# An adaptive-norm and expert network on one core: the first stage's side work reordered (ternary weights, routing, first loads)

## What is computed

```
h  = x @ W_base.T + b + 2 * lora(x; As, Bs, cond)          # 8 adapters of rank 16, weighed per batch row
xn = layernorm(h) * gamma + beta
s  = max|xn| / 127;  xq = round(xn / s) * s                # one scale over the whole tensor
delta = 0.7 * mean|w|;  mask = |w| > delta
alpha = sum(|w| * mask) / max(sum(mask), 1)
x  = x + xq @ (alpha * sign(w) * mask).T                   # ternary weight

w, sel = top2(softmax(cond));  w = w / sum(w)              # router: 2 of 8 experts for each batch row
y  = sum_e w_e * mlp_e(x) + shared_mlp(x)                  # gelu(x Wg) * (x Wu) @ Wd, hidden 512
x  = x + quantised_gated_ffn(y)                            # global maxima between its steps
```

## Time and profile before

| | |
|---|---|
| time of the profiled execution | 493.8 us |
| its span | 491.9 us |
| median of three runs | 493.7 us |
| TensorE busy over the span | 390.9 us (79%) |
| VectorE / ScalarE / GpSimd busy | 336.2 / 267.8 / 254.5 us |
| TensorE busy, 0 to 68 us | 52.5 us |
| VectorE busy, 0 to 68 us | 39.8 us |
| VectorE busy in 28 to 44 us | 15.9 of 16 us |

### The profile page before, as it was taken

The page is one execution under the profiler, slowest core; times in us unless marked ns, Lnnn a source line. Parts: engine busy times, 40 slices in busy tenths (PEclk is TensorE's granted clock), DMA queues, the critical chain, the costliest instruction groups (busy, mean ns, idle before and its releaser), DMA issues.

```text
span 491.9 us, 8519 instructions
## 1 busy us (share of the span) xinstructions
PE 390.9 (79%) x2556; PEld 343.3 (70%) x2556; DVE 336.2 (68%) x564; ACT 267.8 (54%) x403; POOL 254.5 (52%) x444
## 2 busy tenths in 40 slices
PE   3998949999999999999999999798587860000297
PEld 2786636779999999999999998566265640000197
DVE  2697458557888767777677676467465778979643
ACT  3575558755454454544545446354365679659360
POOL 2667426886767756657566102566233018967140
PEclk9998758999999999999999999899588995555599
DMA  8899900228777777676777506200000000000012
GB/s 287 331 311 322 333 3 0 82 91 279 240 249 262 242 264 256 233 278 237 253 261 233 193 23 267 87 1 1 0 0 0 1 0 0 0 1 0 0 65 107
DMA packets 30786, 71.26 MB, mean 145 GB/s; under 512 B 3475, under 2 KB 19606, under 8 KB 25494
## 3 DMA queue, kind: packets, MB, share of 16 engines
...
q10 hardware_dynamic: 1472, 0.20, 0.3%
...
HBM read 55.12 MB, written 15.60 MB: 144 GB/s over the span
## 4 chain that ended last, share of the span: by engine, by line
PE 63%; DVE 18%; ACT 8%; POOL 5%; DMA 4%; issue 2%; ACTq 0%; POOLq 0%; DVEq 0%
PE ps L180 46%; PE ps L734 10%; DVE S L198 7%; DVE G L189 4%; PE ps L737 4%; DMA G<-yscr,sidx 3%; PE ps L177 2%; DMA wbr<-in_L_cond_W_base_dram 2%; ACT ps L186 1%; ACT G L186 1%; POOL Hl L189 1%; POOL XCl L189 1%; ACT U L186 1%; ACT C_i L186 1%; DVE G L195 1%
## 5 line engine op out<-in xcount | busy, mean ns | idle before, releaser
L689 POOL CAST xg<-XT 128x64 fp32r x312 | 115.4, 417 | 59.5 <-PE ps L180 55.8
L186 ACT ACTIVATE Gb<-ps 128x512 f32<-128x512 f32 x110 | 65.7, 597 | 106.4 <-PE ps L180 105.9
L180 PE MATMUL ps<-xg,Wr 128*128 128x256 f32 x936 | 120.0, 284 | 0.0
L189 DVE TENSOR_TENSOR HbS<-Gb,ps 128x512 f32<-128x512 f32 x110 | 75.5, 687 | 63.5 <-PE ps L180 61.8
L180 PEld LDWEIGHTS ps<-xg,Wr 128*128 128x128 f32 x936 | 114.3, 190 | 0.1
L186 ACT ACTIVATE Hh<-HbS 128x512 fp32r<-128x512 f32 x110 | 69.0, 628 | 13.8 <-DVE HbS L189 13.6
L734 PE MATMUL ps<-WD,Hh 128*128 x312 | 74.3, 328 | 0.0
L737 PE MATMUL ps<-WD,Hl 128*128 x312 | 69.4, 223 | 0.0
L189 DVE TENSOR_TENSOR Hl<-HbS,Hh 128x512 fp32r<-128x512 f32 x90 | 64.5, 726 | 2.6
L737 PEld LDWEIGHTS ps<-WD,Hl 128*128 128x128 f32 x312 | 59.8, 192 | 0.0
L734 PEld LDWEIGHTS ps<-WD,Hh 128*128 128x128 f32 x312 | 59.0, 189 | 0.0
(11 more groups left out here) (183 smaller groups left out, 699.8 us busy)
## 6 DMA issues: line engine op xcount, KB each, us to landing
...
yscr<-Yb SPq DMA_DIRECT2D x39, 128.0 KB, 2.7
...
```

Of the source, the lines that this page charges most:

```text
L180: return lambda e: e.matmul(o_, l, r, start=start, stop=stop, skip_group_check=True)
L186: return lambda e: e.activation(o_, i_, func, **kw)
L189: return lambda e: e.tensor_tensor(o_, a, b, op)
L689: k_xg[i] = pool.do(lambda e, s=s: e.tensor_copy(xg[:, i % XR, :, T * s:T * s + T], XT[:, :, :, bass.ds(regb[i][s], 1)].rearrange("p a t o ...
```

## The change

Four things are done, all in the first stage:

1. On ScalarE's transfer queue the order is now `wbr`, `fwr`, `bsr`; `fwr` leaves SyncE's queue. `wbr` gets a place in SBUF of its own beside `grow`.
2. In round 1 the adapter products of tile 0 come ahead of the products of `wbr` and `grow` on TensorE, and `hs` ahead of `WbTl` on VectorE.
3. The ternary chain moves from rounds 5 to 7 into rounds 0 and 1. Mask and masked value come from one operation each (`tpos`, `tsc` and `tneg`, `tsc2`, with -1 in `tneg`), there are four sums instead of two, and the two halves are added in PSUM by two products with `identF`. These and the product of `ones` with the sums stand in round 2 of TensorE. `tern` and `alpha` are made in round 3.
4. `Pm` is made at the end of round 4 (in round 5 before), its product stands in round 5 (6 before), and `ordI` in round 6 (7 before).

```diff
--- before.py
+++ after.py
...
+        tsc2 = at("tsc2", [128, 128], F32)
...
-        l_bs = act.dma(lambda e: e.dma_start(bsr[:, :].rearrange("o (e r) -> o e r", e=E), Bs.rearrange("e o r -> o e r")), s_in[4], 1)
         l_wb = act.dma(lambda e: e.dma_start(wbr[:, :], Wb), s_in[6], 1)
+        l_fw = act.dma(lambda e: e.dma_start(fwr[:, :], fw), s_in[2], 1)
+        l_bs = act.dma(lambda e: e.dma_start(bsr[:, :].rearrange("o (e r) -> o e r", e=E), Bs.rearrange("e o r -> o e r")), s_in[4], 1)
...
             tok["w01"] = dve.do(stt(S[:, 38:40], S[:, 34:36], 1.0 / 12, S[:, 36:38], MUL, ADD), d_)
+            d_f = dve.do(red(S[:, 10:11], fwr[:, :], ADD, True), l_fw)
             yield True
+            p_f = pe.do(mm(bank[6][:, 16:17], ones[:, :], S[:, 10:11], True, True), d_f)
             pe.do(mm(bank[6][:, 0:8], tri[:, :], S[:, 64:72], True, True), d4, k_tri, sig=False)
             p_ = pe.do(mm(bank[6][:, 8:16], ones[:, :], S[:, 64:72], True, True))
+            yield
+            d_ = dve.do(ts(S[:, 44:45], bank[6][:, 16:17], 0.7 / 16384, None, MUL), p_)
+            dve.do(cp(S[:, 72:80], bank[6][:, 0:8]), p_)
+            dve.do(ts(S[:, 80:88], bank[6][:, 8:16], 1.0 / SL, 0.5 - 0.5 / SL, MUL, ADD), p_)
+            d6 = dve.do(ts(S[:, 45:46], S[:, 44:45], -1.0, None, MUL), d_)
+            dve.do(ts(tpos[:, :], fwr[:, :], S[:, 44:45], None, ALU.is_gt), d_)
+            dve.do(stt(tsc[:, :], fwr[:, :], S[:, 44:45], fwr[:, :], ALU.is_gt, MUL), d_)
+            d_n = dve.do(ts(tneg[:, :], fwr[:, :], S[:, 45:46], -1.0, ALU.is_lt, MUL), d6)
+            d7 = dve.do(stt(tsc2[:, :], fwr[:, :], S[:, 45:46], fwr[:, :], ALU.is_lt, MUL), d6)
+            yield
+            dve.do(red(S[:, 46:47], tpos[:, :], ADD), d7)
+            dve.do(red(S[:, 47:48], tsc[:, :], ADD))
+            dve.do(red(S[:, 140:141], tneg[:, :], ADD))
+            d7 = dve.do(red(S[:, 141:142], tsc2[:, :], ADD))
+            yield
+            d7 = dve.do(tt(S[:, 46:48], S[:, 46:48], S[:, 140:142], SUB), d7)
             yield True
...
+            pe.do(mm(bank[6][:, 18:20], ones[:, :], S[:, 46:48], True, True), d7, sig=False)
+            pe.do(mm(bank[6][:, 384:512], tpos[:, :], identF[:, :], True, False), tok["w2"], sig=False)
+            p_t = pe.do(mm(bank[6][:, 384:512], tneg[:, :], identF[:, :], False, True), d_n)
...
+            tok["tern"] = dve.do(cp(tern[:, :], bank[6][:, 384:512]), p_t)
+            d_a = dve.do(ts(S[:, 140:141], bank[6][:, 18:19], 1.0, None, ALU.max), p_t)
             for i in range(1, E):
...
+                if i == 1:
+                    d_a = dve.do(lambda e: e.reciprocal(S[:, 141:142], S[:, 140:141]), d_a)
+                if i == 3:
+                    tok["alpha"] = dve.do(tt(S[:, 142:143], S[:, 141:142], bank[6][:, 19:20], MUL), d_a)
...
-            yield True
+            yield
             dve.do(cp(bcF[:, :], bcI[:, :]), k_bc)
             d_P = dve.do(stt(Pm[:, :], iof[:, :], S[:, 43:44], tmpP[:, :], ALU.is_equal, ADD), (dve.sem, dve.n - 1))
...
             yield True
-            p_ = pe.do(mm(bank[6][0:1, 0:NSLOT], bcF[:, :], Pm[:, :], True, True), d_P)
...
-            yield True
+            p_ = pe.do(mm(bank[6][0:1, 0:NSLOT], bcF[:, :], Pm[:, :], True, True), d_P, tok["alpha"])
+            yield True
             tok["ord"] = dve.do(cp(ordI[:, :], bank[6][0:1, 0:NSLOT]), p_)
-            pe.do(mm(bank[6][:, 18:20], ones[:, :], S[:, 46:48], True, True), d_, tok["ord"], sig=False)
-            p_ = pe.do(tr(bank[6][:, 384:512], tpos[:, :], identF[:, :]), tok["w2"])
...
-            if n == 1:
-                p_ = pe.do(mm(bank[5][:, 0:128], wbr[:, :], ctr[:, :], True, True), l_wb, k_ctr)
...
-            fill(2)
+            if n != 1:
+                fill(2)
...
             if n == 1:
+                p_ = pe.do(mm(bank[5][:, 0:128], wbr[:, :], ctr[:, :], True, True), l_wb, k_ctr)
...
+                fill(1)
                 p_ = pe.do(mm(AV[:, 0:128], bsr[:, :], ctr[:, :], True, True), l_bs)
```

More of the change, by code:

```diff
@@ L121, in program @@
         stg = at("stg", [128, 8, 512], F32)
-        wbr = at("wbr", [128, 128], F32)
         asr = at("asr", [128, 128], F32)
@@ L152, in program @@
         grow = at("grow", [1, 3, 128], F32)
+        wbr = at("wbr", [128, 128], F32)
         assert off[0] <= RQ
@@ L237, in program @@
         l_a0 = act.dma(lambda e: e.dma_start(asr[:, :], As.rearrange("e r c -> (e r) c")), s_in[1], 1)
+        l_wb = act.dma(lambda e: e.dma_start(wbr[:, :], Wb), s_in[6], 1)
+        l_fw = act.dma(lambda e: e.dma_start(fwr[:, :], fw), s_in[2], 1)
         l_bs = act.dma(lambda e: e.dma_start(bsr[:, :].rearrange("o (e r) -> o e r", e=E), Bs.rearrange("e o r -> o e r")), s_in[4], 1)
-        l_wb = act.dma(lambda e: e.dma_start(wbr[:, :], Wb), s_in[6], 1)
         act.do(acp(S[0:1, 15:16], S4[0:1, 40:41], ACT.Exp), d_one)
@@ L247, in program @@
             l_gb = sp.dma(lambda e, k=k, v=v: e.dma_start(grow[0:1, k, :], v.rearrange("(a n) -> a n", a=1)), s_in[5], k + 1)
[L248 to L251, removed]
+        for n in range(8):
             load_w(n)
@@ L350, in route @@
             d_ = dve.do(stt(S[:, 96:104], S[:, 96:104], float(SL), S[:, 72:80], MUL, ADD), d_)
-            yield True
-            p_f = pe.do(mm(bank[6][:, 16:17], ones[:, :], S[:, 10:11], True, True), d_f)
             for i in range(1, E - 1):
@@ L463, in program @@
             if n == 1:
+                p_ = pe.do(mm(bank[5][:, 0:128], wbr[:, :], ctr[:, :], True, True), l_wb, k_ctr)
+                a_ws[0] = act.do(acp(WbTh[:, :], bank[5][:, 0:128]), p_)
+                d_ws[0] = dve.do(tt(WbTl[:, :], bank[5][:, 0:128], WbTh[:, :].bitcast(F32), SUB), a_ws[0])
+                for k in range(3):
+                    p_ = pe.do(mm(AZ[:, k:k + 1], grow[0:1, k, :], S4[0:1, 40:41], True, True), l_gb, d_one, sig=(k == 2))
+                d_ = dve.do(cp(S[:, 8:10], AZ[:, 0:2]), p_)
+                d_bb = dve.do(cp(S[:, 143:144], AZ[:, 2:3]), p_)
+                fill(1)
                 p_ = pe.do(mm(AV[:, 0:128], bsr[:, :], ctr[:, :], True, True), l_bs)
```

7 lines of the change are left out of this document (1 added, 6 removed).

## The result

The changed kernel takes 499.06 us, the median of five runs from 498.0 to 500.36. The kernel before takes 493.7 beside it (five runs, 489.41 to 496.85). The ratio is 1.0139, with a 95% interval of 1.009 to 1.0188, so the change makes the kernel 4.4 to 9.3 us slower. The ratio compares fast runs alone and leaves the one of 496.85 us out, which is why it gives 6.9 us where the medians lie 5.4 apart. The profiled execution of after took 499.06 us with a span of 497.3, against 493.8 and 491.9: the span is 5.4 us longer. The forecast of 497.3 us had the direction and lay 1.8 us short of this median; by the ratio the loss is 6.9 us where 3.6 were forecast.

The account below looks back on a forecast made before the run. TensorE was taken to bound the first stage, whose delays reach the end whole. Terms of +1.7 (front and ternary), +4.8, -4.6 and +1.7 gave +3.6 us, so 497.3 us, range 490.8 to 500.5.

Parts of the forecast that it names:

- front: Start up to round 2: splits behind `stg` still set the pace, so new load and work order win only -0.3 us.
- ternary wait and products: Round 2: TensorE waits 1.1 us for the ternary sums, then three new products take 0.9 us.
- order product: Round 5: TensorE waits 4.1 us for `Pm`, and its product of 0.69 us comes to this round; +4.8 us.
- recovery: Round 5's correction to round 9: no product waits for `ordI`, undisturbed pace if the clock stays high; -4.6 us.
- clock: Round 5: TensorE's granted clock falls to 0.50 behind the longer wait, in place of round 7's fall; +1.7 us.
- wait for `Pm`: Round 5: TensorE asks for `Pm` 11.4 us behind round 3's base product, ready at 15.5, so waits 4.1 us.
- `Pm` is in time: Faster rival: VectorE loses little to splits in rounds 3 and 4, clock holds; -2.2 us, 491.5, or 489; chance 0.22.
- a short wait and no fall: No-change rival: a 2.5 us wait for `Pm` in round 5, clock holds or falls briefly; +0.4 us, 494.1; chance 0.24.
- late first rise of the clock: Slower rival: the wait at 19.0 us makes TensorE's clock rise one round later; +2 to the forecast, 499.5; chance 0.16.

Follow-up runs that it names:

- e2: The changed kernel with `Pm`'s product moved to round 6 and `ordI` to round 7; 491.97 us, ratio 0.9996.
- e9: The changed kernel with 13 unused products of 512 columns on TensorE ahead of `Pm`'s product in round 5; 496.6 us, ratio 1.0109.
- e1: The changed kernel with `bsr` loaded ahead of `wbr` and `fwr` on ScalarE's queue; 498.82 us, ratio 1.016.
- e4: The changed kernel with the three ternary products in round 3 instead of 2, `tern` and `alpha` later in round 3; 496.72 us, ratio 1.0099.
- e5: The kernel before with only the order part: `Pm` made at the end of round 4, its product in round 5; 498.92 us, ratio 1.0137.
- e3: The changed kernel with `bcF` and `Pm` ahead of the two `etI` operations on VectorE in round 4; 497.34 us, ratio 1.0108.
- e6: The kernel before with only round 1's new order, adapter products ahead of `wbr`'s, loads as before; 490.4 us, ratio 0.9959.
- e8: The changed kernel with `Pm`'s product in round 6, ternary products in round 3, loads as before, and weight splits a round later; 491.73 us, ratio 1.0022.
- e7: The changed kernel with `Pm`'s product in round 6, ternary products in round 3, and loads as in the kernel before; 490.7 us, ratio 0.9999.

## Why the prediction was right in its direction and short in its size

The shift at the start of round 9 is 60.71 - 54.89 = 5.8 us. Put beside the terms:

| term | forecast | measured | how |
|---|---|---|---|
| front | -0.3 | +1.4 | 17.58 - 16.21 |
| ternary wait and products | +2.0 | +1.7 | 6.85 - 5.19; wait 0.84, products 0.69 |
| rounds 3 and 4 | 0 | 0 | 9.64 each |
| order product | +4.8 | +3.9 | wait 3.19 + 0.69 |
| recovery | -4.6 | -5.4 | 23.85 - 18.42 |
| clock | +1.7 | +4.3 | 26.64 - 18.42 - 3.88 |
| sum | +3.6 | +5.8 | |

The sum is taken from unrounded terms. 18.42 us is the undisturbed pace of rounds 5 to 8: two rounds of 4.82, and two of 4.39, since no tile is left to transpose on the way to the starts of rounds 8 and 9. In e2 these two took 8.78 us (54.88 - 46.10). The clock's term is what is left when pace, wait and product are taken off, so other small delays would be in it; e9 found 4.2 by another way.

**The step that failed is "The clock".** I saw that the longer wait would bring the fall to round 5. I priced it at 1.7 us by what rounds 7 and 8 had lost before, with a bound of 3.4 from the 6.8 us that the low clock lasted there. It lasted 10.2 us and cost 4.3, above that bound. Two things were wrong in it. I took 4.82 us as the pace of rounds 7 and 8, where it is 4.39: they were 13.26 - 8.78 = 4.48 us above their pace in the kernel before, not 3.6, so the fall had cost 2.6 us even there. In the sum this one cancels, since the recovery was larger by the same 0.9 us. And I took the length of the low stretch as fixed; this is the rest of the miss, 4.34 - 2.56 = 1.8 us. In the four kernels in which the fall began inside the wait (3.19 us in after and e1, 3.91 in e4, 2.99 in e5) it lasted 10.2 us. Where it began in the work behind a shorter wait it lasted 6.8 (before with 1.42 us, e3 with 2.21) or 3.4 (e6 with 1.42, e8 with 1.13). Behind the waits of 0.82 and 0.74 us in e2 and e7 there was no fall. Why the lengths differ is not settled: it is an order seen in ten profiles, the same 1.42 us was followed by 6.8 and by 3.4, and no run varied the wait alone.

**The front** was the second miss, in its mechanism too. I took the splits behind `stg` as what sets round 2. But in every kernel TensorE works from the product of the load it waited for to round 2 without a wait of over 0.1 us: 5.85 us behind `wbr`'s product in before and e5, 4.72 in e6, 4.99 in e1 and e7, 5.14 in e8, and 1.62 or 1.63 behind `bsr`'s in after, e2, e3, e4 and e9. ScalarE had `WbTh` ready long before:

```profile
12.66 0.27 ACT L186 ACTIVATE WbTh<-ps 128x128 fp32r<-128x128 f32 x1
```

In this timeline of the kernel before that is 3.3 us ahead of its product at 16.21, and TensorE had worked without a gap from 10.36 on, not only from 15.46 as I had read. So the last load that TensorE needs sets the front. The wait for `wbr` did go, and I never asked when `bsr`, which was put last, would land, though its product stands right ahead of round 2. In after it landed 13.2 us after its issue, against 7.4 before. But the +1.4 us isn't the change's alone. Over the executions round 2 started at 16.21, 17.52, 19.93, 16.11, 17.44 and 15.34 with `bsr` ahead of `wbr` (before, e1, e5 to e8), and at 17.58, 16.67, 16.64, 17.62 and 17.11 with `bsr` last (after, e2, e3, e4, e9): means of 17.1 and 17.1. By these eleven profiles the order of the loads moves the front no more than it moves from one execution to the next.

**Right were** the ternary wait (1.1 forecast, 0.84 found; two operations were held by the splits as laid out, though `tneg` in place of `tsc`) and the wait for `Pm`, with 3.19 us where 4.1 were forecast. It was asked for 11.4 us behind round 3's base product, as forecast (35.87 - 24.43), and was ready at 14.6 instead of 15.5: `xTl` of round 4 started 7.1 us behind that product and not 7.6, and the rest of the way took 7.5 and not 7.9. Most of the lateness was there already: 14.2 us in the kernel before, and 14.2 in e5 without the ternary chain's operations in round 3. From the maximum on nothing changed, as forecast. Of the rivals, "`Pm` is in time" and "a short wait and no fall" are refuted by the trace. The late first rise of the clock did not happen in after, but it did in e3 and e9. That the total lies close to the forecast owes something to luck: the front was 1.7 us worse than forecast, the order product and the ternary wait 1.2 us better.
